# Rotation, local attentions and feed-forward stages of a two-layer block written as one program on each engine

## Chip, cores and metric

One core of a Trainium2 chip runs the whole kernel. The metric is the device time of one execution in microseconds (us), of which the median over several runs is compared. The engines are PE (TensorE, matmuls), DVE (VectorE), ACT (ScalarE), POOL (GpSimd) and SP, which here only issues DMAs. Each has its own queue of instructions that it runs in order, and waits in it on semaphores.

## What is computed

The input x is (2, 1024, 256), so 2 batches of T = 1024 tokens with D = 256 features. A first layer (a 16-head attention and a mixture of 64 experts) makes x1. Then x1 goes through a rotation, which is one 256 x 256 matrix, and through two local transformer layers, and is added again. The change touches only this second half:

```python
for l in range(2):                      # _L1_ffn_ref, q/k scales and norm weights left out
    h = shift_token(x)                  # second half of the features comes from the token before
    q, k, v = split(h @ wqkv[l], 3)     # 8 heads of 64
    q, k = rotary_xpos(l2norm(q), l2norm(k))
    o = local_attention(q, k, v)        # windows of 128: a window sees itself and the one before
    x = x + o @ wo[l]
    h = shift_token(x)
    h = (h - mean(h)) / sqrt(var(h) + 1e-5) * lg + lb
    a, g = split(h @ w1[l] + b1[l], 2)  # 682 value columns, 682 gate columns
    x = x + (a * gelu(g)) @ w2[l] + b2[l]
```

## The kernel before

The second half is five stages, each a block of its own: `stage_rotate` (line 1222), `stage_attention1` for layer 0 (line 1331), `stage_ffn1` for layer 0 (line 1716), and the two again for layer 1. At the end of a block every engine waits for all others, so no instruction of a stage starts before the last of the stage before it. Tokens lie in `xr`, features on the partitions, with one zero column ahead of each batch, so that `shift_token` is only an offset.

**Precision.** Products that need it are split: an operand is a high part (rounded to fp32r) and a low part (what is left), and three matmul products (`PRODUCTS`: high*high, high*low, low*high) make one. So a weight has to be split by copying to the low tile on ACT, subtracting on POOL or DVE, and rounding on ACT (lines 1199 to 1219 for `wqkv`).

**Rotation.** For 16 tiles t of 128 tokens, DVE scales the output of the experts (`r_on`, line 1267), PE transposes it (line 1294), DVE adds it to the input (`r_x1T`, line 1273). After every fourth tile, PE multiplies a block of 512 tokens by the rotation (`rotate`, line 1285), and ACT copies it to `xr` (line 1311). Besides this ACT and POOL split `wqkv` of layer 0 (lines 1203, 1211, 1219), POOL scales the rotary tables (line 1327), and SP writes x1 to HBM in 4 parts (line 1249), which the last stage reads again.

**Attention.** There are 16 windows (NG) of 128 tokens and 20 slots t. Five windows are in work in a slot, in an order written out by hand for each engine. In slot t:
- PE: `rows_of(t-2)` (transposes of q and k, line 1482), `queries_keys(t)` (12 matmuls, line 1460), `scores(t-2, 0)`, `prob_rows(t-3, 0..1)` (line 1506), `mixed(t-4)` (output projection, line 1525), `values(t)` (6 matmuls, line 1460), `prob_rows(t-3, 2..3)`, `scores(t-2, 1)` (line 1497), `weighted(t-3)` (line 1516).
- ACT: q, k and output copies, `w_qkr` (line 1571) and `w_sq` (line 1573) out of the bank of q and k, exponentials (line 1588), a square root of norms in odd slots (line 1597).
- DVE: masked maxima (line 1663), sums of squares (line 1646), `w_sinp` (the sine term, line 1640), copies of transposed probabilities (line 1676), the residual add (line 1681), the split of tokens `w_hst` (lines 1631 and 1633).
- POOL: `w_cosp` (line 1420), `w_turned` (lines 1429 and 1435), the scaling of the probabilities (line 1413).

PE can't start `rows_of(0)` before window 0 has been through the whole chain PE, ACT, DVE and POOL, and POOL normalises windows 0 and 1 together, after both.

**Feed-forward.** Four units (2 batches, 2 halves) of 512 tokens, in a loop over the batches. A unit is 6 hidden tiles f of 128 columns, each with a gate and a value half of 6 matmuls (line 1855), then 36 matmuls of w2 (line 1869). The 682 columns are padded to 768, so there are 12 column tiles. The norm of the unit that follows is made beside it: a matmul for the mean and one for the variance on PE (lines 1833 and 1837), `m_xc` (line 1943), reciprocals `m_rs` (line 1948) and rounding (line 1965) on DVE, squares (line 1886), root `m_sd` (line 1891) and scaling (line 1897) on ACT, and `m_xn` and the low part (lines 1803 and 1806) on POOL. The last unit of a layer makes such a norm too, of a unit that nothing uses. The first unit's norm is made at the start of the stage, with PE waiting. There ACT and DVE split w1 (lines 1901, 1958) and POOL splits w2 (lines 1809, 1811). In layer 0, ACT and POOL then split `wqkv` of layer 1, ahead of the first gelu (line 1921) in ACT's order.

Of the kernel before, what the change touches and what calls it, by code (L numbers as in the profile page):

```python
# [22 lines left out]
F32 = mybir.dt.float32  # L23
# [5 lines left out]
ds = bass.ds  # L29
# [37 lines left out]
HIDP = FT * P  # L67
QK_SCALE = 8.0
# [1120 lines left out]
def load_ffn1(sp, G, A, l):  # L1189
    sp.dma_start(G["w1"][:, :, :], A["w1"][l].rearrange("(k p) n -> p k n", p=P)).then_inc(G["ld_ffn"], 16)  # L1190
    sp.dma_start(G["w2"][:, :, :], A["w2"][l].rearrange("(k p) n -> p k n", p=P)).then_inc(G["ld_ffn"], 16)
    for name in ("lg", "lb", "b1", "b2"):
        sp.dma_start(G[name][:, :], A[name][l]).then_inc(G["ld_ffn"], 16)


LD_ATT, LD_FFN = 32, 96


def copy_wqkv(nc, act, G, l):

    act.wait_ge(G["ld_att"], LD_ATT * (l + 1))
    for k in range(KD):
        nc.scalar.activation(G["wqkv1"][1][:, k, :], G["wqkv1_raw"][:, k, :], ACT.Copy).then_inc(G["wqkv_copy"], 1)


def split_wqkv(nc, pool, G, l):

    low = G["wqkv1"][1]
    for k in range(KD):
        pool.wait_ge(G["wqkv_copy"], KD * l + k + 1)  # L1210
        nc.gpsimd.tensor_tensor(low[:, k, :], G["wqkv1_raw"][:, k, :], low[:, k, :].bitcast(F32),
                                ALU.subtract).then_inc(G["wqkv_low"], 1)


def round_wqkv(nc, act, G, l):

    for k in range(KD):
        act.wait_ge(G["wqkv_low"], KD * l + k + 1)
        nc.scalar.activation(G["wqkv1"][0][:, k, :], G["wqkv1_raw"][:, k, :], ACT.Copy).then_inc(G["wqkv_high"], 1)


def stage_rotate(nc, G, A):


    with ExitStack() as ctx:
        sb = lambda n, s, dt=F32: ctx.enter_context(nc.sbuf_tensor(n, s, dt))
        sem = lambda n: ctx.enter_context(nc.semaphore("r_" + n))
        PB, ident, xr = G["PB"], G["ident"], G["xr"]
        TILES = B * TT
        x1T = sb("r_x1T", [P, KD, N])  # L1230
        rden = sb("r_rden", [P, TILES])
        on = sb("r_on", [P, 2, D])
        step, on_ready, t_ps, x1_done, rot_ps, rot_out, zeroed = (sem(n) for n in (
            "step", "on_ready", "t_ps", "x1_done", "rot_ps", "rot_out", "zeroed"))
        ld_x = [sem(f"ld_x{n}") for n in range(N // HALF)]
        with nc.Block() as block:
            @block.sync
            def _(sp):
                for n in range(N // HALF):
                    ts = slice(n * HALF, (n + 1) * HALF)  # L1240
                    sp.dma_start(x1T[:, :, ts], A["xT"].rearrange("(k p) n -> p k n", p=P)[:, :, ts]).then_inc(ld_x[n], 16)
                load_attention1(sp, G, A, 0)
                sp.dma_start(G["mask"][:, :], A["mask"]).then_inc(G["ld_tab"], 16)
                sp.dma_start(G["qks"][:, :, :, :], A["qks"]).then_inc(G["ld_tab"], 16)
                load_tables(sp, G, A)
                for n in range(N // HALF):
                    ts = slice(n * HALF, (n + 1) * HALF)
                    sp.wait_ge(x1_done, 4 * n + 4)
                    sp.dma_start(G["x1"].rearrange("(k p) n -> p k n", p=P)[:, :, ts], x1T[:, :, ts]).then_inc(G["x1_out"], 16)
                sp.wait_ge(G["x1_out"], 16 * (N // HALF))  # L1250

            @block.gpsimd
            def _(pool):
                nc.gpsimd.memset(xr[:, :, :, 0:1], 0.0).then_inc(zeroed, 1)
                split_wqkv(nc, pool, G, 0)
                scale_tables(nc, pool, G, 0)

            @block.vector
            def _(dve):
                V = nc.vector  # L1260
                link = chain(dve, step)
                link(V.reciprocal(rden[:, :], G["den"][:, :]))
                for t in range(TILES + 1):
                    if t < TILES:
                        if t >= 2:
                            dve.wait_ge(t_ps, t - 1)
                        V.tensor_scalar_mul(on[:, t % 2, :], G["O"][:, t, :], rden[:, t:t + 1]).then_inc(on_ready, 1)
                    if t >= 1:
                        r = t - 1
                        if r * P % HALF == 0:  # L1270
                            dve.wait_ge(ld_x[r * P // HALF], 16)
                        dve.wait_ge(t_ps, r + 1)
                        V.tensor_tensor(x1T[:, :, r * P:(r + 1) * P],
                                        PB[0][:, HALF * (r % 2):HALF * (r % 2) + D].rearrange("p (k t) -> p k t", k=KD),
                                        x1T[:, :, r * P:(r + 1) * P], ALU.add).then_inc(x1_done, 1)

            @block.tensor
            def _(pe):
                def rotate(n):
# [899 lines left out]
```

## Time and profile before

| | us |
|---|---|
| median of 3 runs | 1647.94 |
| lowest and highest | 1646.35, 1648.55 |
| the profiled execution | 1648.95 |
| its span, first to last instruction | 1647.2 |
| mean granted TensorE clock | 0.969 of full speed |

The span is divided by the profile into busy and idle time of each engine. A line of the timeline gives start, duration, engine, line of the kernel, output and inputs, and how many instructions were merged in it. In brackets stands how long the engine was idle before it, and which instruction ended that. The second half of the kernel begins at about 869 us of the span, the attention of layer 0 at 904, its feed-forward at 1141, the attention of layer 1 at 1274, and its feed-forward at 1513.

### The profile page before, as it was taken

To read this page: it belongs to the slowest core of one execution; us is meant where nothing else is said; L and a number is where in the kernel's file an instruction comes from. 1 tells how busy PE (TensorE), PEld (TensorE's weight loads), DVE (VectorE), ACT (ScalarE), POOL (GpSimd) and SP (SyncE) were. 2 spreads that over 40 slices of the span, in tenths; PEclk is the share of its full clock that TensorE was granted. 3 is DMA by queue.
4 is the path that set the end of the run, shared out by engine and by line. 5 is a ranking of instruction groups with operands and counts; after the bars stand their busy time and mean duration, and the time that the engine had idled before them with its cause. 6 is when DMAs were issued, how large, how long until landed. Compare 5 with 4: busy or idle time off the path is not lost. (4 is left out here: it accounts for less than half of the span.)

```text
span 1647.2 us, 24889 instructions
## 1 busy us (share of the span) xinstructions
PE 1498.2 (91%) x9060; PEld 983.4 (60%) x9060; DVE 1050.9 (64%) x1915; ACT 903.6 (55%) x1870; POOL 503.4 (31%) x313
## 2 busy tenths in 40 slices
PE   8889999999986999999996699997799699997898
PEld 3432222222234888888883477775677577775676
DVE  3768888888637656565654456555777455555786
ACT  5147777777751434343432577775443577776342
POOL 7100000000015100000002587774412587774223
PEclk9999999999999999999998899999899799999899
DMA  8831212200000330303006100003000100000010
GB/s 245 141 39 20 34 26 40 40 2 1 11 14 12 120 104 13 103 13 103 0 0 191 55 1 1 1 2 77 1 1 4 54 1 1 2 1 26 4 48 26
DMA packets 59472, 64.98 MB, mean 39 GB/s; under 512 B 15154, under 2 KB 48706, under 8 KB 59380
## 3 DMA queue, kind: packets, MB, share of 16 engines
q1 hardware_dynamic: 58020, 60.37, 14.7%
q10 hardware_dynamic: 1360, 3.41, 0.6%
q8 instruction: 55, 0.90, 0.2%
q14 instruction: 37, 0.30, 0.1%
HBM read 53.08 MB, written 10.49 MB: 39 GB/s over the span
## 5 line engine op out<-in xcount | busy, mean ns | idle before, releaser
L578 DVE TENSOR_REDUCE mcol<-bank 128x1 f32<-128x1024 f32 x256 | 301.8, 1217 | 58.0 <-PE bank L569 58.0
L666 ACT ACTIVATE a_pt<-bank 128x512 f32<-128x512 f32 x512 | 266.1, 603 | 88.2 <-PE bank L698 88.2
L698 PE MATMUL bank<-qa,ka 99*128 99x512 bf16 x512 | 192.9, 384 | 7.6 <-ACT a_pt L666 3.8
L569 PE MATMUL bank<-ka,qa 96*128 96x512 bf16 x512 | 192.4, 383 | 6.4 <-DMA ka<-k_parts 2.9
L1663 DVE CUSTOM_DVE_ANT_0 w_sm<-bank,mask 128x256 f32<-128x256 f32 (+1 forms) x256 | 89.0, 404 | 147.6 <-PE bank L1497 147.6
L1855 PE MATMUL bank<-m_hn,m_w 128*128 128x512 f32 x576 | 150.9, 419 | 19.0 <-DVE m_hn L1986 16.4
L1460 PE MATMUL bank<-wqkv,w_hst 128*128 128x512 f32 x576 | 156.6, 420 | 12.5 <-DVE w_sinp L1640 7.6
L698 PEld LDWEIGHTS bank<-qa,ka 99*128 99x128 bf16 x512 | 49.1, 98 | 165.1 <-ACT a_pt L666 120.7
L1855 PEld LDWEIGHTS bank<-m_hn,m_w 128*128 128x128 f32 x576 | 112.3, 195 | 56.1 <-issue 27.2
L709 PE MATMUL bank<-a_pt,vst 128*32 128x512 f32 x1024 | 136.4, 605 | 0.1
L1588 ACT ACTIVATE w_sm<-w_sm,w_st 128x256 f32<-128x256 f32 (+1 forms) x256 | 124.0, 489 | 19.2 <-DVE w_st L1663 19.0
L1460 PEld LDWEIGHTS bank<-wqkv,w_hst 128*128 128x128 f32 x576 | 109.6, 199 | 37.6 <-issue 14.9
L1413 POOL TENSOR_TENSOR w_sm<-w_sm,w_st 128x1024 f32<-128x1024 f32 (+1 forms) x64 | 114.8, 1794 | 37.3 <-DVE w_st L1670 37.3
L1064 PE MATMUL bank<-f_y,f_ET 128*128 128x256 f32 x768 | 108.6, 290 | 0.7 <-DVE f_y L1163 0.7
L615 POOL COPY vst<-v 128x512 f32<-128x512 f32 x8 | 4.9, 612 | 334.8 <-PE bank L709 278.2
L1064 PEld LDWEIGHTS bank<-f_y,f_ET 128*128 128x128 f32 x768 | 96.1, 191 | 3.9 <-issue 1.6
L1420 POOL TENSOR_TENSOR w_cosp<-w_qkr,cosT 128x1024 f32<-128x1024 f32 x32 | 75.9, 2373 | 67.0 <-ACT w_qkr L1571 67.0
L1021 PE MATMUL bank<-phi,X0T 128*128 128x512 f32 x384 | 92.1, 394 | 3.9 <-PEq L765 3.9
L995 PE MATMUL bank<-f_th,X 128*128 128x512 f32 x384 | 90.3, 389 | 0.0
L1429 POOL TENSOR_TENSOR w_turned<-w_cosp,w_sinp 128x1024 f32<-128x1024 f32 x32 | 75.7, 2366 | 43.5 <-issue 34.0
L569 PEld LDWEIGHTS bank<-ka,qa 96*128 96x128 bf16 x512 | 49.6, 98 | 62.6 <-DVE mcol L578 11.5
L1021 PEld LDWEIGHTS bank<-phi,X0T 128*128 128x128 f32 x384 | 73.0, 191 | 19.8 <-issue 4.7
(236 smaller groups left out, 2688.8 us busy)
## 6 DMA issues: line engine op xcount, KB each, us to landing
f_wex<-in_W SPq DMA_DIRECT2D x8, 2048.0 KB, 12.0
qa<-q_parts SPq DMA_DIRECT2D x48, 128.0 KB, 4.8
ka<-k_parts SPq DMA_DIRECT2D x48, 128.0 KB, 5.1
q_parts<-p_parts SPq DMA_DIRECT2D x16, 192.0 KB, 3.2
k_parts<-p_parts SPq DMA_DIRECT2D x8, 384.0 KB, 3.5
wqkv_raw<-in_wqkv SPq DMA_DIRECT2D x2, 1536.0 KB, 8.7
w<-in_w SPq DMA_DIRECT2D x2, 1536.0 KB, 6.5
phi<-in_phi SPq DMA_DIRECT2D x5, 512.0 KB, 3.7
```

Of the source, the lines that this page charges most:

```text
L569: last = nc.tensor.matmul(max_bank(G, r)[:, jh * HALF:(jh + 1) * HALF], G["qa"][k][0:KS, hg % 2, h, it * P:(it + 1) * P], G["ka"][k][0:KS, ...
L578: nc.vector.reduce_max(G["mcol"][hg % 2][:, p:p + 1], max_bank(G, r)[:, :], X).then_inc(G["max_free"], 1)
L666: nc.scalar.activation(pt[n % 2][:, q, :], sbank(HG * step + q), ACT.Exp, scale=HD0 ** -0.5).then_inc(p_ready, 1)
L698: mm(sbank(i), ka[k][:, q, n * P:(n + 1) * P], qa[k][:, ih, q, :], start=True, stop=True).then_inc(st_ps, 1)
L709: last = mm(obank[32 * q:32 * q + 32, :], vst[hg // 2 % 2][:, jt, q, :], pt[jt % 2][:, q, :], start=(jt == 0), stop=(jt == TT - 1))
L995: last = mm(PB[2 + b][:, k * HALF:(k + 1) * HALF], X0[cx][:, b * TT + mt, k * P:(k + 1) * P], ths[ct][:, mt % 2, :], start=(mt == n == 0), ...
L1021: last = mm(logit_bank(mt)[:, b * HALF:(b + 1) * HALF], X0T[cx][:, k, b * T + mt * P:b * T + (mt + 1) * P], phis[cp][:, k, :], start=(n == ...
L1064: last = mm(PB[1][:, HALF * (t % 2):HALF * (t % 2) + D], ETs[ce][:, t % 2, n, :], ys[cy][:, n, t // TT, :], start=(n == i == 0), stop=(n = ...
L1413: V.tensor_tensor(sm[:, i % 2, hs, keys(i)], sm[:, i % 2, hs, keys(i)], st[:, i % 2, 3, hs].unsqueeze(2).to_broadcast([P, 4, 2 * WIN if i ...
L1460: last = mm(out, hst[:, i // 2 % 2, ch, k, (i % 2) * P:(i % 2 + 1) * P], wqkv[cw][:, k, j * INNER:(j + 1) * INNER], start=(n == k == 0), s ...
L1588: last = S(sm[:, i % 2, h, keys(i)], sm[:, i % 2, h, keys(i)], ACT.Exp, bias=st[:, i % 2, 1, h:h + 1], scale=-1.0, accum_out=st[:, i % 2, ...
L1855: last = mm(PB[2 + f % 2][:, part * HALF:(part + 1) * HALF], w1s[cw][:, k, col + f * P:col + (f + 1) * P], hns[ch][:, hf, k, :], start=(n ...
```

## The change

The five stages become one block, `stage_layers`, with one written-out program on each engine and no loop instructions. The parts:
- Windows 0 and 1 of layer 0 (`EARLY_SLOTS` = 2) are projected among the rotation's tiles, after tiles 9 and 13. Those of layer 1 are projected inside the last unit of the feed-forward of layer 0. The attention program then begins at slot 2.
- The norm of a layer's first unit is made in slots 15 to 19 of its attention. No norm is made beside the last unit.
- w1 and w2 are split in 3 pieces within the attention's slots 5 to 11 (ACT copies in slots 5 to 7, POOL subtracts in 7 to 9, ACT rounds in 9 to 11). DVE no longer takes part in it. `wqkv` of layer 1 is split after units 0 and 1.
- The last 42 value and 42 gate columns of w1 share one tile of 128 columns, so a unit has 11 column tiles instead of 12.
- Values are kept for 5 windows and keys for 2, in rings. The mask has three parts, so that an odd and an even window find their keys in the ring's order.
- Loads of the following layer's weights and tables are issued by SP after waits on what read the ones before. x1 is read again, and the output stored, a half at a time.

```diff
+VRING = 5
+EARLY_SLOTS = 2
...
+        def w1_cols(f):
+            return (WHOLE * P + f * P, f * P) if f < WHOLE else (2 * WHOLE * P,)
...
             @block.gpsimd
...
                     for t in SLOTS1:
...
+                        if 7 <= t < 7 + NPIECES:
+                            low_piece(l, t - 7)
...
+                attention(0)
+                normalise(0)
+                normalise(1)
+                for k in range(KD):
+                    low_qkv(1, k)
+                normalise(2)
+                for i in range(4):
+                    scale_table(1, i)
+                normalise(3)
+                attention(1)
...
             @block.tensor
...
+                    for t in SLOTS1[first:]:
+                        if there(t - 2):
+                            rows_of(t - 2)
+                        if there(t):
+                            queries_keys(l, t)
+                        if t == NG:
+                            pe.wait_ge(qk_sb, before(NG))
+                            pe.wait_ge(sin_done, before(NG))
+                            means(UNITS * l)
...
+                        if there(t - 3):
+                            prob_rows(t - 3, 2)
+                            prob_rows(t - 3, 3)
+                        if t == NG:
+                            variances(UNITS * l)
+                        if there(t - 2):
+                            scores(t - 2, 1)
...
+                def feed_forward(l):
+                    for n in range(UNITS):
...
+                        for f in range(FT):
...
+                            if ahead and f in (1, 3):
+                                queries_keys(l + 1, f // 2)
+                            if ahead and f in (2, 4):
+                                values(l + 1, f // 2 - 1)
+                        pe.wait_ge(y_done, KD * u)
+                        if ahead:
+                            pe.wait_ge(qk_sb, NG * (l + 1) + EARLY_SLOTS)
+                            pe.wait_ge(sin_done, NG * (l + 1) + EARLY_SLOTS)
...
+                for t in range(TILES):
+                    turn_rows(t)
+                    if t % 4 == 1 and t >= 4:
+                        rotate(t // 4 - 1)
+                    if t in (9, 13):
+                        queries_keys(0, t // 4 - 2)
+                        values(0, t // 4 - 2)
+                rotate(TILES // 4 - 1)
+                pe.wait_ge(x1_done, TILES)
+                pe.wait_ge(rot_out, KD * (N // HALF))
+                pe.wait_ge(G["x1_out"], 16 * (N // HALF))
+                attention(0, EARLY_SLOTS)
...
             @block.scalar
...
+                        if t == NG:
+                            squares(UNITS * l)
...
+                        if 5 <= t < 5 + NPIECES:
+                            copy_piece(l, t - 5)
+                        if 9 <= t < 9 + NPIECES:
+                            round_piece(l, t - 9)
+                        if t == NG + 1:
+                            deviation(UNITS * l)
+                        if t == NG + 2:
+                            scaled(UNITS * l)
...
+                for n in range(N // HALF):
+                    if n == 1:
+                        copy_qkv(0)
+                    rotated(n)
+                    if n == 1:
+                        round_qkv(0)
+                    if n >= 2:
+                        queries_keys(0, n - 2)
+                        values(0, n - 2)
+                norms(0, 0)
...
             @block.vector
...
+                        if t == NG:
+                            centred(UNITS * l)
...
+                        if t == NG - 1:
+                            tile_sums(UNITS * l)
...
+                        if t == NG:
+                            square_sums(UNITS * l)
+                        if there(t - 3):
+                            prob_rows(t - 3, 2)
...
+                        if t == NG + 2:
+                            for q in range(2):
+                                inverse(UNITS * l, q)
+                    high(UNITS * l)
...
+                    if t == 9:
+                        dve.wait_ge(zeroed, 1)
+                        split_tokens(0, 0)
+                    if t == 13:
...
+                        squared_norms(0, 0)
+                        sines(0, 0)
+                split_tokens(0, 1)
+                squared_norms(0, 1)
+                sines(0, 1)
+                inverse_norms(0, 0)
```

Names of the new program that the diff shows: `rotated(n)` is ACT's copy of a rotated block, `queries_keys` on ACT makes `w_qkr` and `w_sq`, `deviation` is the root `m_sd`, `inverse` the reciprocals `m_rs`, `scaled` makes `m_hn`, and `high` and `normalise` make its two parts.

## Rows read from the trace of the kernel before

**Rows 1.** Page, part 1: busy time of PE, share, instructions.

```profile
PE 1498.2 (91%) x9060; PEld 983.4 (60%) x9060; DVE 1050.9 (64%) x1915; ACT 903.6 (55%) x1870; POOL 503.4 (31%) x313
```

**Rows 2.** Windows of 25 us: length; busy us of PE, PEld, DVE, ACT, POOL; clock; DMA.

```profile
975.00:1000.00 25.00, 24.70 (x204) 20.23 (x204) 13.76 (x47) 19.31 (x49) 18.82 (x10) 1.00 0.01 2
...
1225.00:1250.00 25.00, 25.00 (x105) 19.51 (x104) 18.82 (x25) 9.57 (x13) 5.47 (x4) 1.00 0.00 0
```

**Rows 3.** The chain that ended last, feed-forward of layer 1: start, us, what.

```profile
1530.84 5.24 PE bank L1855 x12
...
1560.18 2.80 PE bank L1855 x12
...
1563.84 8.39 PE bank L1855 x36
...
1589.87 0.86 PE bank L1833 x2
```

**Rows 4.** Timeline of PE, feed-forward of layer 0 and start of layer 1.

```profile
1158.84 5.22 PE L1855 MATMUL bank<-m_hn,m_w 128*128 128x512 f32 x12 [8.20 <-DVE m_hn L1986]
...
1170.28 7.41 PE L1855 MATMUL bank<-m_hn,m_w 128*128 128x512 f32 x24 [2.56 <-DVE m_hid L1997]
...
1192.38 2.96 PE L1855 MATMUL bank<-m_hn,m_w 128*128 128x512 f32 x12
...
1246.16 2.96 PE L1855 MATMUL bank<-m_hn,m_w 128*128 128x512 f32 x12
...
1275.80 5.99 PE L1460 MATMUL bank<-wqkv,w_hst 128*128 128x512 f32 x18 [2.59 <-DVE w_hst L1633]
...
1298.27 1.97 PE L1482 MATMUL bank<-ident,w_turned 128*128 128x128 f32 x8 [7.29 <-POOL w_turned L1435]
```

**Rows 5.** Timelines of DVE, ACT and POOL, end of layer 1's attention and the norms after.

```profile
1507.29 0.69 DVE L1676 COPY w_PT<-bank 128x512 f32<-128x512 f32 x1
...
1515.30 1.28 DVE L1943 TENSOR_TENSOR m_xc<-xr,bank 128x512 f32<-128x512 f32 x2 [1.38 <-PE bank L1833]
...
1523.40 3.37 DVE L1948 RECIPROCAL m_rs<-m_sd 128x256 f32<-128x256 f32 x2 [1.08 <-ACT m_sd L1891]
...
1516.02 1.23 ACT L1886 ACTIVATE m_sq<-m_xc 128x512 f32<-128x512 f32 x2 [1.52 <-DVE m_xc L1943]
...
1552.76 2.73 POOL L1803 TENSOR_TENSOR m_xn<-m_xc,m_rs 128x512 f32<-128x512 f32 x2 [34.00 <-DVE m_rs L1948]
```

**Rows 6.** Timeline of ACT in a unit of layer 0: a table load and what follows.

```profile
1179.29 1.28 ACT L1921 ACT_TABLE_LOAD   x1
1180.59 0.69 ACT L1921 ACTIVATE m_gl<-bank,b 128x512 f32<-128x512 f32 x1
```

**Rows 7.** Timeline of PE, rotation and first slots of layer 0.

```profile
884.07 3.60 PE L1285 MATMUL bank<-r_x1T,rot 128*128 128x512 f32 x8
...
905.74 4.43 PE L1460 MATMUL bank<-wqkv,w_hst 128*128 128x512 f32 x18 [2.30 <-DVE w_hst L1633]
...
926.98 1.97 PE L1482 MATMUL bank<-ident,w_turned 128*128 128x128 f32 x8 [7.62 <-POOL w_turned L1435]
```

**Rows 8.** Timelines of POOL, DVE and ACT in the same stretch.

```profile
885.24 6.87 POOL L1211 TENSOR_TENSOR wqkv<-wqkv_raw,wqkv 128x1536 fp32r<-128x1536 f32 x2 [15.94 <-ACT wqkv L1203]
...
922.73 2.34 POOL L1429 TENSOR_TENSOR w_turned<-w_cosp,w_sinp 128x1024 f32<-128x1024 f32 x1 [1.31 <-DVE w_sinp L1640]
925.02 3.76 POOL L1435 TENSOR_TENSOR w_turned<-w_turned,w_rn 128x1024 f32<-128x1024 f32 x2
...
889.09 3.17 DVE L1267 TENSOR_SCALAR r_on<-O,r_rden 128x256 f32<-128x256 f32 x1
...
912.01 1.22 DVE L1640 TENSOR_TENSOR w_sinp<-bank,sinT 128x1024 f32<-128x1024 f32 x1
...
899.21 2.85 ACT L1219 ACTIVATE wqkv<-wqkv_raw 128x1536 fp32r<-128x1536 f32 x2
...
908.80 1.02 ACT L1571 ACTIVATE w_qkr<-bank 128x1024 f32<-128x1024 f32 x1 [4.73 <-PE bank L1460]
```

More of the change, by code:

```diff
@@ L1193, in load_ffn1, with load_tables @@
         sp.dma_start(G[name][:, :], A[name][l]).then_inc(G["ld_ffn"], 16)
+def load_tables(sp, G, A):
+    for i in range(4):
+        sp.dma_start(G["tab"][i % 2][:, :, i // 2, :], A["tables"][i].rearrange("(w p) d -> p w d", p=P)).then_inc(G["ld_tables"], 16)
 LD_ATT, LD_FFN = 32, 96
[L1199 to L1203, printed above, removed]
@@ L1206, in split_wqkv @@
[L1206 to L1219, printed above, removed]
@@ new lines, in _ @@
+                V.memset(xr[:, :, :, 0:1], 0.0).then_inc(zeroed, 1)
+                V.memset(mean[:, :], 1.0 / D).then_inc(consts, 1)
+                V.memset(eps[:, :], LN_EPS).then_inc(consts, 1)
+                pool.wait_ge(consts, 2)
+                for k in range(KD):
+                    low_qkv(0, k)
+                for i in range(4):
+                    scale_table(0, i)
+                attention(0)
+                normalise(0)
+                normalise(1)
+                for k in range(KD):
+                    low_qkv(1, k)
@@ L1301, in _ @@
-            @block.scalar
-            def _(act):
-                for n in range(N // HALF):
-                    if n == 1:
-                        copy_wqkv(nc, act, G, 0)
-                    if n == 3:
-                        round_wqkv(nc, act, G, 0)
-                    for m in range(KD):
-                        act.wait_ge(rot_ps, KD * n + m + 1)
-                        c0 = 1 + (n % 2) * HALF
-                        nc.scalar.activation(xr[:, m, n // 2, c0:c0 + HALF], PB[1 + m][:, 0:HALF],
-                                             ACT.Copy).then_inc(rot_out, 1)
-                act.wait_ge(zeroed, 1)
@@ L2018, in program @@
+                feed_forward(0)
+                attention(1, EARLY_SLOTS)
+                feed_forward(1)
 def program(nc, A, out):
@@ L2038, in program @@
         G["early_sem"] = early_sem
-        layer_sems = {}
-        def layer_sem(n):
-            if n not in layer_sems:
-                layer_sems[n] = top.enter_context(nc.semaphore(n))
-            return layer_sems[n]
-        G["layer_sem"] = layer_sem
         G["ident"] = sb("ident", [P, P])
@@ L2122, in constants @@
     i, j = np.arange(WIN)[:, None], np.arange(WIN)[None, :]
-    c["mask"] = np.concatenate([np.where(j >= i, 0.0, MASKED), np.where(j <= i, 0.0, MASKED)], 1).astype(f)
+    last, own = np.where(j >= i, 0.0, MASKED), np.where(j <= i, 0.0, MASKED)
+    c["mask"] = np.concatenate([last, own, last], 1).astype(f)
     c["ident"] = np.eye(P, dtype=f)
```

1311 lines of the change are left out of this document (661 added, 650 removed).

## Prediction

> **What bounds the kernel now.** I read the page first: PE is busy 1498.2 of 1647.2 us, the next engine 1050.9 [rows 1]. So time is gained by fewer matmuls or by less idling of PE, and I looked for both in the second half, which the change alone touches. The windows show two kinds of steady work. In a slot of the attention PE has 24.70 of 25 us, while ACT has 19.31 and POOL 18.82 and so some 6 us each to spare. In a unit of the feed-forward PE has all of 25.00 and DVE 18.82 [rows 2]. The chain of waits confirms it for the last stage: PE and nothing else from 1530.84 on, one unit after another [rows 3]. PE idles where the stages meet. That is read from PE's timeline, from landmark to landmark: from the transposes of window 0 back to the block before. These landmarks, not busy shares, carry the sum.
>
> **Fewer matmuls.** 36 matmuls of one kind take 8.39 us, or 0.233 each [rows 3]. A unit loses 6 of them, 1.40 us. The last unit of each layer loses the matmuls for a mean and a variance too, 2 x 0.86 = 1.72 [rows 3]. Seven units here (the eighth is in the next part) give 7 x 1.40 + 1.72 = 11.5 gained. PE is the bound in them, so it counts in full.
>
> **From feed-forward 0 to attention 1.** Before, unit 3 starts at 1246.16 and the first transposes of window 0 at 1298.27 [rows 4]: 52.1 us, in which the two early slots take 36 matmuls (8.4 us if PE is never throttled) and the rest is the round through ACT, DVE and POOL. After, the unit holds 66 + 36 + 36 matmuls of 0.233 = 32.2. I follow its queues. The two projections come after tiles 1 and 3. ACT takes `w_qkr` and `w_sq` between gelus (1.02 each), DVE the sums of squares and the sine term (1.22 each) behind the hidden parts of tiles 2 and 4 [rows 8]. The second projection waits for the first sine term, which comes in time. The w2 matmuls use its bank, and wait for the second: projection ends, ACT 2.0, DVE's tile 4 and 2.4 more. I get 1.5 us of stall. Behind the last w2 matmul stay one residual add and a reciprocal on DVE (1.1) and one POOL multiplication, half of 3.76 [rows 8]: 3.1. Sum 36.8, so 15.3 gained.
>
> **Unit 0 of layer 0.** It takes 33.54 us before (1158.84 to 1192.38), with PE idle 2.56 us at 1170.28 [rows 4], because the gelu stands behind the split of `wqkv` in ACT's queue. The same unit of layer 1 takes 1560.18 - 1530.84 = 29.34 [rows 3]. The split moves behind the unit, so 4.2 are gained. What is late next is the split itself: POOL's two subtractions (6.87 together [rows 8]) now run in the first tiles of unit 1, beside DVE.
>
> **The norm in the last slots.** Before, unit 0's norm stands in the open, begun only when the attention is over, and the unit of layer 1 starts at 1530.84 [rows 3]. After, four things are queued behind new work.
> 1. Slot 16: the variance matmuls wait for centring 1.28, squares 1.23 and their sum, and the second half of the scores is behind them. Between 0.9 (the matmuls alone) and 3.2 (all in the open) I take 2.4, since maxima and exponentials share those queues.
> 2. Slot 17: a table load and the root, 1.28 + 0.69 [rows 6], ahead of the output copy of window 14, on which PE's projection waits: 2.0.
> 3. Slot 18: so the probability copy that ends at 1507.98 [rows 5] ends at 1512.4. Then come the reciprocals, 3.37, and POOL's two products, 2.73: 1518.5.
> 4. ACT's scaling stands ahead of the output copy of window 15. Scaling 0.8, copy 0.6, projection 2.05 and residual add 0.4 give 1522.4. Only then come DVE's rounding and POOL's low parts: 3.1, so the unit starts at 1525.7.
>
> That is 5.1 earlier than 1530.84. Layer 0 ends in the same orders, so 10.2 for both. The bounds for each are 0 (the norm costs the slots what it saves) and 12 (steps 1 and 2 hidden, 4.4, and copy, projection and add, 3.0, not behind the scaling).
>
> The table load is where a page speaks against this. The trace shows 1.28 us and the next activation 0.02 us behind it, though the load starts at once after work [rows 6]. The Trainium skill, ScalarE: Activation LUTs, section "What ACT_TABLE_LOAD costs", adds a drain of about 1.38 us to every switch; by it step 2 would be 3.4 us instead of 2.0, and the sum 2.8 smaller over two layers. I go by the row.
>
> **Early slots among the rotation.** This looks like a gain and is, by the queues, a loss. Before, PE is through with block 1 of the rotation at 887.7, and the first transposes of window 0 run at 926.98 [rows 7]. After:
> - The first projection stands behind tile 9, but needs `wqkv` split: POOL is done at 892.1 and ACT's rounding 1.4 later [rows 8], so 893.5. PE has idled 6 us. In the trace 18 matmuls take 4.43 us after a short idle time, 5.99 after others, and 12 take 5.22 after 8.20 idle [rows 4, 7]. I take 6.6, to 900.1.
> - Tiles 10 to 13 and block 2: 6, to 906.2. ACT copies block 2 before q and k, 0.7, then 2.0. DVE's squares and sine term 2.4: 911.4. The second projection waits for that.
> - Projection 6, tiles 14 and 15 with DVE's adds 1.8, block 3 3.6 [rows 7]: 922.9.
> - ACT block 3 0.7, q and k 2.0, DVE 2.6; POOL's sum 2.34 and product 1.9 [rows 8]: 932.4.
>
> So 5.5 us lost. The bounds are 2 (PE keeps its clock) and 8. The write of x1 isn't the last wait: its last DMA starts when tile 15 is added, about 919, so it has 13 us. Before, the same DMA, tiles 10 to 15 and two blocks all fitted between 887.7 and 905.74 [rows 7].
>
> **Splitting the weights inside the slots.** Per layer POOL gets 3 subtractions of up to 3.4 us and ACT 6 copies of up to 1.45, for which I use the `wqkv` rows of 1536 columns [rows 8]. Each slot gets one of a kind. Their cover is the idle quarter of both engines [rows 2], and what they delay (probabilities, q and k copies) is used half a slot later. At nothing they would cost 0; with no cover, 2 x (3 x 3.3 + 6 x 1.4) = 37. I take 1 us a layer: 2 lost.
>
> **The port.** DVE's scaling `r_on` took 3.17 us instead of 0.34 because POOL's subtraction ran [rows 8]. In unit 1, DVE's casts meet POOL's two. PE waits only for the first of DVE's three steps of a tile, from PSUM, so 1 us is lost. The Trainium skill, GPSIMD Engine Reference, section "Specifications", says that POOL shares its SBUF interface with DVE; the row agrees.
>
> **Sum.** 11.5 + 15.3 + 4.2 + 10.2 - 5.5 - 2 - 1 = 32.7 us gained. The profiled execution took 1648.95, so 1616.3; it is 1.0 above the median of 1647.94, which gives 1615.3.
>
> **Rivals.**
> - *Norm and early slots hide fully.* If ACT's scaling doesn't hold up window 15 and steps 1 and 2 are hidden, each norm gives 7.4 more, and if the early slots fit in PE's waits the 5.5 are not lost: 20.3 more, 1595. For it speaks that waits that I add one behind another may overlap. Against it, the orders on ACT. Chance 0.15.
> - *The ends are given back.* The norm's steps lengthen the last slots by all they save (10.2 less), and the rotation costs 8 (2.5 more): 1628. Chance 0.18.
> - *The splits are on the path (the slower side).* POOL and ACT close a ring with PE in each slot. The place is slots 5 to 11, and the port makes DVE late too. With no cover the cost is 37 instead of 2: 1650. It decides slower above 2.1 us per piece, for 18 pieces. The spare 6 of 25 us [rows 2] speak against it. Chance 0.04.
> - *The early slots do not do what they say.* If the bank that q, k and w2 share makes PE wait in unit 3 for both rounds through ACT and DVE, 2 x (2.0 + 2.4) come on top, 8.8: 1624. Chance 0.08.
>
> My forecast has 0.55. The range, 1602 to 1630, holds the forecast, its own bounds, the second and fourth rival, and leaves out the first and third. A measurement of this kernel tells 0.2% (3.3 us) from no change. Below 1644.6 lie all cases but the third and something unseen: faster 0.94, same 0.02, slower 0.04.
>
> **What would show it.** In the profile after: w1 matmuls 528 instead of 576; units of about 25.5 us; window 0's transposes of layer 1 about 37 us after the start of unit 3; those of layer 0 later than 927, with PE idle before the first projection for `wqkv`; feed-forward starts 5 us earlier after the last slot, with PE waiting for ACT's output copy in front of the last projection. The prediction is wrong if slots 5 to 11 are longer than the others, if w2 waits long for a sine term, or if PE's clock falls inside a unit.

## Result and the profile after

The changed kernel takes 1633.86 us (median of 4 runs, 1631.24 to 1635.53). The kernel before takes 1647.24 beside it (4 runs, 1646.35 to 1648.55). The ratio is 0.9914, with an interval of 0.9901 to 0.9926. So it is faster, as forecast, but by 13.4 us instead of 32.7, and 1633.86 lies above the forecast range of 1602 to 1630.

First the page of the changed kernel, part 1, which answers to [rows 1], and its windows, which answer to [rows 2]. The first window is one slot of layer 0 that stands out.

```profile
PE 1493.2 (92%) x9004; PEld 975.4 (60%) x9004; DVE 1028.7 (63%) x1879; ACT 897.9 (55%) x1854; POOL 514.6 (32%) x313
```

```profile
1020.00:1037.00 17.00, 14.66 (x109) 11.84 (x106) 11.57 (x27) 11.81 (x28) 15.70 (x8) 0.90 0.01 1
975.00:1000.00 25.00, 24.15 (x202) 19.73 (x202) 13.69 (x48) 21.37 (x48) 20.24 (x10) 1.00 0.01 2
1225.00:1250.00 25.00, 24.85 (x103) 18.53 (x102) 20.21 (x29) 9.62 (x13) 5.47 (x4) 1.00 0.00 1
```

PE's busy time fell by 5.0 us only, and it is still the bound nearly everywhere. In the slot that stands out, slot 9, PE is idle for 2.3 of 17 us, its mean clock is 0.90 and POOL is busy for 15.70. The experiments e4 and e5 look for the reason.

The profiled execution took 1631.24 (span 1629.5), 17.7 less than the 1648.95 before. It is the fastest of its four runs. I divided the 17.7 by landmarks of PE's timeline, those of the prediction:

| stretch | before | after | gained | forecast |
|---|---|---|---|---|
| start to the rotation's first transposes | 869.93 | 867.79 | 2.1 | 0 |
| from there to window 0's transposes | 57.05 | 60.95 | -3.9 | -5.5 |
| to window 14's, both layers | 370.7 | 377.4 | -6.7 | -2 |
| window 14's to unit 0, both layers | 93.7 | 88.7 | 5.1 | 10.2 |
| layer 0, unit 0 to unit 3 | 87.32 | 83.45 | 3.9 | 7.4 |
| unit 3 to window 0's transposes | 52.11 | 38.79 | 13.3 | 15.3 |
| layer 1, unit 0 to the last w2 matmuls | 101.46 | 97.93 | 3.5 | 7.3 |
| from there to the end | 14.9 | 14.5 | 0.4 | 0 |

The first 2.1 us lie ahead of anything that changed. They are no effect of it: another execution of the changed kernel reached the same point at 869.69. Without them the trace shows 15.6, and five of the seven forecasts are too high. One profiled execution gives such a stretch to about 1 us: the norm's stretch, for one, takes from 43.4 to 45.0 us a layer in the eight profiled executions whose program is the same there. Here is PE's timeline of the changed kernel. These lines answer to [rows 7]:

```profile
881.65 3.60 PE L1524 MATMUL bank<-r_x1T,rot 128*128 128x512 f32 x8
891.42 6.04 PE L1539 MATMUL bank<-wqkv,w_hst 128*128 128x512 f32 x18 [6.18 <-ACT wqkv L1716]
...
908.02 6.22 PE L1539 MATMUL bank<-wqkv,w_hst 128*128 128x512 f32 x18 [5.09 <-DVE w_sinp L1910]
...
928.74 1.94 PE L1567 MATMUL bank<-ident,w_turned 128*128 128x128 f32 x8 [9.73 <-POOL w_turned L1463]
...
1031.54 1.94 PE L1590 MATMUL bank<-ident,w_sm 128*128 128x128 f32 x8 [2.34 <-DVE w_PT L1983]
1033.41 1.83 PE L1581 MATMUL bank<-w_kT,w_qT 64*128 64x256 f32 x8
...
1271.93 9.18 PE L1681 MATMUL bank<-m_hid,w 128*128 128x512 f32 x36 [2.00 <-DVE w_sinp L1910]
1284.26 1.97 PE L1567 MATMUL bank<-ident,w_turned 128*128 128x128 f32 x8 [3.15 <-POOL w_turned L1463]
...
1497.95 2.79 PE L1609 MATMUL bank<-w_oT,wo 128*128 128x128 f32 x16 [2.21 <-ACT w_oT L1792]
1500.54 1.91 PE L1590 MATMUL bank<-ident,w_sm 128*128 128x128 f32 x8
...
1509.54 3.56 PE L1609 MATMUL bank<-w_oT,wo 128*128 128x128 f32 x16 [5.16 <-ACT w_oT L1792]
1517.07 5.49 PE L1659 MATMUL bank<-m_hn,w 128*128 128x512 f32 x12 [3.97 <-POOL m_hn L1425]
...
1563.51 9.53 PE L1681 MATMUL bank<-m_hid,w 128*128 128x512 f32 x36
```

The reader is to see six things. The projections among the rotation wait for `wqkv` and for the first sine term (891.42, 908.02). Slot 9 has an idle time that the kernel before did not have, and its next two groups run slowly (1031.54, 1033.41; the same groups take 1.06 and 1.13 in other slots). In unit 3, w2 waits 2.00 us for a sine term. Both late output projections wait for ACT's `w_oT` and are slow (2.79, 3.56). w2's 36 matmuls, which I had at 8.4, take 9.53. And the feed-forward of layer 1 starts at 1517.07.

ACT's timeline at the end of layer 1's attention shows what the last two projections wait for:

```profile
1495.43 1.28 ACT L1768 ACT_TABLE_LOAD   x1
1496.73 0.69 ACT L1768 ACTIVATE m_sd<-bank,m_eps 128x512 f32<-128x512 f32 x1
1497.31 0.59 ACT L1792 ACTIVATE w_oT<-bank 128x512 f32<-128x512 f32 x1
...
1508.20 0.82 ACT L1776 ACTIVATE m_hn<-m_xn,lb,lg 128x512 f32<-128x512 f32 x1 [0.36 <-POOL m_xn L1422]
1508.92 0.58 ACT L1792 ACTIVATE w_oT<-bank 128x512 f32<-128x512 f32 x1
```

Window 14's copy stands behind the table load and the root, window 15's behind the second scaling, though its data were ready at 1504.4.

### The profile page after: what moved, and what is told of

It is laid out like the page before. It is cut to its first block and busy times, and to the rows that moved or that the text cites. A ratio compares the mean times of both kernels' runs of the same rounds, so it can differ in the third digit from the quotient of the medians.

```text
span 1629.5 us, 24376 instructions
## 1 busy us (share of the span) xinstructions
PE 1493.2 (92%) x9004; PEld 975.4 (60%) x9004; DVE 1028.7 (63%) x1879; ACT 897.9 (55%) x1854; POOL 514.6 (32%) x313
## 5 line engine op out<-in xcount | busy, mean ns | idle before, releaser
L1659 PE MATMUL bank<-m_hn,w 128*128 128x512 f32 x528 | 137.1, 416 | 8.0 <-issue 4.0
L1659 PEld LDWEIGHTS bank<-m_hn,w 128*128 128x128 f32 x528 | 102.0, 195 | 39.2 <-issue 12.2
L1848 ACT ACTIVATE m_gl<-bank,b 128x512 f32<-128x512 f32 (+1 forms) x48 | 33.1, 689 | 104.3 <-PE bank L1659 104.3
L1590 PE MATMUL bank<-ident,w_sm 128*128 128x128 f32 x480 | 68.9, 288 | 20.5 <-DVE w_PT L1983 20.5
```

Of the source, the lines that this page charges most:

```text
L1590: last = tr(T_PS[p % 2][:, c0:c0 + P], sm[:, i % 2, 2 * p + e, j * P:(j + 1) * P], ident[:, :])
L1659: last = mm(PB[2 + f % 2][:, part * HALF:(part + 1) * HALF], w1s[cw][:, k, col:col + P], hns(u)[:, ch, k, :], start=(i == k == 0), stop=(i ...
```

## Experiments

Unless it is said otherwise, each is one edit of the changed kernel. The gain is given against the first run here, and every median can be off by about 1 us. All kernels before measured beside them had medians of 1647.1 to 1648.1.

| run | median us | ratio to before | gain |
|---|---|---|---|
| changed kernel again | 1631.55 | 0.9901 [0.9886, 0.9916] | |
| e1 full rows | 1629.06 | 0.9886 [0.9869, 0.9902] | 2.5 |
| e2 half tiles grouped | 1629.94 | 0.9894 [0.9877, 0.991] | 1.6 |
| e3 copy before scaling | 1621.33 | 0.9843 [0.9827, 0.986] | 10.2 |
| e4 subtract in odd slots | 1625.38 | 0.9864 [0.9848, 0.9881] | 6.2 |
| e5 subtract in even slots | 1628.28 | 0.9881 [0.9866, 0.9896] | 3.3 |
| e6 no early slots in layer 0 | 1626.43 | 0.9876 [0.9861, 0.9891] | 5.1 |
| e7 = e1 + e3 + e4 + e6 | 1605.93 | 0.9742 [0.9729, 0.9755] | 25.6 |
| e8 full rows and grouped | 1628.74 | 0.989 [0.9875, 0.9905] | 2.8 |
| e9 = e3 + earlier reciprocals | 1620.45 | 0.9837 [0.9821, 0.9852] | 11.1 |
| e10 = e7 + e8 + earlier reciprocals | 1604.4 | 0.9733 [0.972, 0.9747] | 27.2 |
| e11 = e10 + earlier variance | 1601.07 | 0.9719 [0.9706, 0.9732] | 30.5 |

**The changed kernel again**, without an edit, as the level for the others.

> The changed kernel itself, with nothing altered, beside the runs that follow. It shows how far its time moves between sessions: 1633.9 us was measured first, and sums over its landmarks in one profiled execution say some 1631. A time of 1630 to 1634 is expected; the gains of the other kernels are read against both.

It took 1631.55 (1630.79 to 1633.37). Slot 9 takes 17.02 and 16.94 us in it (17.02 and 16.92 in the first profile), and the middle units 26.6. The pattern is the program's, not one execution's.

**e1: w2's last hidden tile in 128 rows.** The tile of the last 42 columns has 64 rows in the changed kernel. Here PE and DVE take 128. The rows of w2 that the other 64 meet are zero, so they add nothing to the sum.

```diff
-mm(..., w2s[cw][value_rows(f), f, m * P:(m + 1) * P], hids[ch][value_rows(f), f, :], ...)
+mm(..., w2s[cw][:, f, m * P:(m + 1) * P], hids[ch][:, f, :], ...)
...
-v, s, r = FT * u + f, f % 2, value_rows(f)
+v, s, r = FT * u + f, f % 2, slice(0, P)
```

> The last hidden tile goes through w2 with all 128 rows (the upper 64 meet zero weights) instead of 64. Theory, switch: a matmul of 64 rows next to one of 128 keeps the weight load from running beside the matmuls, and this makes 36 w2 matmuls take 9.5 us instead of 8.4. Then each unit of the feed-forward is 1.05 us shorter (unit 1 of layer 1: 26.6 to 25.5) and the kernel 8.4 us faster. Rival, late tile: w2 waits for DVE's last hidden tile. Then it stays at 9.5 and the time doesn't move.

It gave 2.5 us, not 8.4. Middle units went from 26.60 to 26.20. The weight loads of the changed kernel show why anything was gained:

```profile
1569.40 0.54 PEld L1681 LDWEIGHTS bank<-m_hid,w 128*128 128x128 f32 x3 [0.58 <-DVE m_hid L2040]
1570.30 0.52 PEld L1681 LDWEIGHTS bank<-m_hid,w 64*128 64x128 f32 x3 [0.37 <-issue]
1571.18 0.53 PEld L1681 LDWEIGHTS bank<-m_hid,w 128*128 128x128 f32 x3 [0.36 <-issue]
1572.07 0.53 PEld L1681 LDWEIGHTS bank<-m_hid,w 64*128 64x128 f32 x3 [0.37 <-issue]
1572.96 0.19 PEld L1659 LDWEIGHTS bank<-m_hn,w 128*128 128x128 f32 x1 [0.36 <-issue]
```

Three loads of 64 rows take as long as three of 128 (0.52, 0.53). But at each change of the row count the next load starts 0.37 us late, behind no wait. So the smaller tile saves no load time here and costs at its borders. The Trainium skill, TensorE: Matmul & The Clock Gate, section "LDWEIGHTS (loading the stationary operand)", says that the time of a load depends on its columns, not its rows; the rows agree. The first line shows a second loss, a wait for DVE. In e1 it is still there (PEld's timeline of e1):

```profile
1570.17 2.62 PEld L1681 LDWEIGHTS bank<-m_hid,w 128*128 128x128 f32 x12 [0.60 <-DVE m_hid L2040]
```

**e2: w2 in three groups**, so that the 64-row matmuls stand together and the last wait comes later.

```diff
-for tiles in (range(FT - 2), range(FT - 2, FT)):
+for tiles in (range(FT - 2), range(FT - 2, FT - 1), range(FT - 1, FT)):
```

> Still 64 rows, but the six matmuls of 64 rows stand together at the end of a unit, so there are 2 changes of row count per unit instead of 4. If the price is per change, w2 falls from 9.5 to 9.0 us and the kernel is 4 us faster. If it is per matmul of 64 rows (0.18 us on each of 6), nothing moves. If the last tile was late, nothing moves either.

It gave 1.6. w2 takes 8.74 instead of 9.53 and its wait is gone, yet the unit takes 26.18: PE now waits at the next unit's start, for POOL's low part of the norm (0.29 at 1571.85). Middle units can't separate the two losses, since e1 and e2 both end at 26.2. Unit 3 of layer 0 can: there w2 starts 2.00 us after the matmuls before it, behind a sine term, and never waits for the last hidden tile. In the changed kernel w2, with three changes of the row count inside it, takes 9.18. PE's timelines of e1 (no change) and e2 (one change):

```profile
1273.26 8.61 PE L1681 MATMUL bank<-m_hid,w 128*128 128x512 f32 x36 [2.00 <-DVE w_sinp L1910]
```

```profile
1273.59 8.81 PE L1681 MATMUL bank<-m_hid,w 128*128 128x512 f32 x36 [2.01 <-DVE w_sinp L1910]
```

That is 0.2 us for each change. So of the 9.53 in a middle unit some 0.6 are the three changes, and by difference to 8.5 some 0.4 the wait for DVE (an estimate).

**e3: window 15's output copy ahead of the norm's scaling on ACT.**

```diff
-                        if t == NG + 2:
+                        if t == NG + 3:
                             scaled(UNITS * l)
```

> ACT's scaling of the first norm moves behind the output copy of window 15 (slot 19 instead of 18). Theory, ACT's queue: PE idles 5.1 us before the last output projection because the copy stands behind the scaling. Then the projection starts some 7 us earlier, and the unit starts when the low parts are ready, 5 us earlier in each layer: 10 us faster in all. Rival, the norm's own chain (reciprocals, products, scaling, rounding, low parts) ends no earlier: the projection moves, the unit starts at most 1 us earlier, and the time gains 2 us or less.

It gave 10.2, as much as expected. PE's timeline of e3 at the end of layer 1's attention:

```profile
1494.46 2.05 PE L1609 MATMUL bank<-w_oT,wo 128*128 128x128 f32 x16 [2.21 <-ACT w_oT L1792]
1496.35 1.04 PE L1590 MATMUL bank<-ident,w_sm 128*128 128x128 f32 x8
1497.32 1.97 PE L1600 MATMUL bank<-w_PT,w_vsb 128*64 128x128 f32 x32
1499.98 2.05 PE L1609 MATMUL bank<-w_oT,wo 128*128 128x128 f32 x16 [0.70 <-ACT w_oT L1792]
1507.20 4.52 PE L1659 MATMUL bank<-m_hn,w 128*128 128x512 f32 x12 [5.17 <-POOL m_hn L1425]
```

From window 14's transposes to unit 0 it takes 39.00 and 37.91 instead of 44.36 and 44.30. The wait of 5.16 before the last projection is 0.70, and the projection takes 2.05 instead of 3.56. Copy, projection and residual add no longer stand between the scaling and the rounding.

Not all of this is the order. PE's granted clock also fell in the changed kernel and not in e3. These are windows of the changed kernel and then of e3; the clock is the third value from the end:

```profile
1492.75:1497.95 5.20, 2.99 (x42) 2.58 (x40) 2.24 (x10) 4.59 (x12) 3.25 (x2) 1.00 0.00 0
1497.95:1502.40 4.45, 4.45 (x26) 4.12 (x26) 1.19 (x3) 0.44 (x1) 0.00 (x0) 0.63 0.02 4
```

```profile
1489.26:1494.46 5.20, 2.99 (x42) 2.58 (x40) 2.24 (x10) 4.58 (x12) 3.25 (x2) 1.00 0.00 0
1494.46:1497.30 2.84, 2.84 (x24) 2.69 (x24) 0.74 (x2) 0.44 (x1) 0.00 (x0) 1.00 0.03 6
```

The work ahead is the same in both, to the hundredth on PE. Then the changed kernel runs at a mean of 0.63 and e3 at 1.00. This first fall is no effect of the order: e7, which has e3's order, has it too (2.73 and 1.91 us for the same two groups), and its stretch to unit 0 is 39.02 in layer 1, 1.1 more than e3's. The last projection is another matter. In the changed kernel it follows 5.16 us of idle time and its clock is 0.54 (1509.50 to 1513.00); in e3 and e7 it follows 0.70 us and takes 2.05. So the order gives 5.3 of the 6.4 us in layer 1.

In unit 3 of layer 0, which e3's edit does not touch, e3 loses 1.6: the clock falls inside w2, which takes 10.76 us at 1266.97. In e4, e5, e6 and e9 this stretch is as long as in e3 (40.4 from unit 3's start to window 0's transposes, changed kernel 38.8). So up to some 2 us of any single gain can be where the clock falls.

**e4 and e5: POOL's subtractions of w1 and w2 in every second slot** instead of the neighbouring slots 7, 8 and 9; ACT's roundings move with them. In e4 they are in odd slots, behind the scaling of two windows of q and k on POOL, in e5 in even ones.

```diff
-                        if 7 <= t < 7 + NPIECES:
-                            low_piece(l, t - 7)
+                        if t in (7, 9, 11):
+                            low_piece(l, (7, 9, 11).index(t))
...
-                        if 9 <= t < 9 + NPIECES:
-                            round_piece(l, t - 9)
+                        if t in (9, 11, 13):
+                            round_piece(l, (9, 11, 13).index(t))
```

(e5 has 8, 10, 12 and 10, 12, 14.)

> POOL's three subtractions per layer stand after slots 7, 9 and 11 instead of 7, 8 and 9 (ACT's roundings after 9, 11 and 13). Slot 9 took 17.0 us instead of 13.6 in each layer. Theory, pile-up or collision behind the subtraction of slot 8: with none there slot 9 falls back to 13.6 and the kernel is 6.8 us faster. Rival, each subtraction has a price wherever it is: the 3.4 us are only spread over more slots and the time stays within 2 us.

> POOL's three subtractions stand after slots 8, 10 and 12, one slot apart from each other, each after an even slot. Theory, phase: after an even slot a single subtraction moves POOL's cosine product of the odd slot onto the small DVE operation w_nsq, which needs the shared port (it took 1.99 us instead of 0.18), and the probability copies behind it make PE wait. Then slots 9, 11 and 13 each take up to 3.4 us more, and the kernel is 10 to 14 us slower than with subtractions after odd slots. Rival, pile-up: only two subtractions in neighbouring slots are too much for POOL; then the time is that of the odd placement.

e4 gave 6.2: slot 9 takes 13.64 again, and no slot from 5 to 13 shows a cost of the splits. e5 gave 3.3, between the theories: slot 9 takes 14.10 and slot 13 takes 14.39, instead of one slot of 17.02. DVE's and POOL's timelines of the changed kernel, slots 8 and 9:

```profile
1026.43 1.22 DVE L1916 TENSOR_REDUCE w_ss<-w_sq 128x16 f32<-128x1024 f32 x1
1027.67 1.99 DVE L1919 TENSOR_SCALAR w_nsq<-w_ss 128x32 f32<-128x32 f32 x1
1029.58 1.21 DVE L1910 TENSOR_TENSOR w_sinp<-bank,sinT 128x1024 f32<-128x1024 f32 x1
1030.72 0.68 DVE L1983 COPY w_PT<-bank 128x512 f32<-128x512 f32 x1
```

```profile
1021.79 3.65 POOL L1416 TENSOR_TENSOR w<-w_raw,w 128x1408 fp32r<-128x1408 f32 x1
1025.39 1.90 POOL L1440 TENSOR_TENSOR w_sm<-w_sm,w_st 128x1024 f32<-128x1024 f32 x1
1027.24 2.39 POOL L1449 TENSOR_TENSOR w_cosp<-w_qkr,cosT 128x1024 f32<-128x1024 f32 x1
```

After PE's wait of 2.34 in slot 9 the clock falls too (window of the changed kernel, clock 0.55):

```profile
1031.50:1035.20 3.70, 3.66 (x18) 2.79 (x18) 1.26 (x4) 1.67 (x2) 3.70 (x3) 0.55 0.00 0
```

And the same DVE and PE groups in e4:

```profile
1030.74 0.18 DVE L1919 TENSOR_SCALAR w_nsq<-w_ss 128x32 f32<-128x32 f32 x1
```

```profile
1032.79 1.06 PE L1590 MATMUL bank<-ident,w_sm 128*128 128x128 f32 x8 [0.53 <-DVE w_PT L1983]
1033.79 1.13 PE L1581 MATMUL bank<-w_kT,w_qT 64*128 64x256 f32 x8
```

With two subtractions in neighbouring slots POOL doesn't catch up, and its `w_cosp` (1027.24) falls on DVE's `w_nsq`, an instruction of 32 elements on each partition. That takes 1.99 instead of 0.18 and ends when POOL's instruction ends (1029.6). Everything behind it on DVE is 1.8 late, the copy `w_PT` too. PE waits 2.34 instead of 0.53, and its next two groups, at the lower clock, lose another 0.88 and 0.70. The sum is 1.81 + 1.58 = 3.4, the whole excess of slot 9. In e5 `w_nsq` takes 0.64 and PE's wait is 0.99, with no slow matmuls behind. So most of the loss is the pile-up (2.2 of the 3.4 us in a layer, by the slots), and the rest is in which slots they stand.

**e6: layer 0's first two windows after the rotation, as before.**

```diff
-                    if t in (9, 13):
-                        queries_keys(0, t // 4 - 2)
-                        values(0, t // 4 - 2)
...
-                attention(0, EARLY_SLOTS)
+                attention(0, 0)
```

> The projections of windows 0 and 1 of layer 0 no longer stand among the rotation's tiles; the attention starts at slot 0 after the rotation, as before the change. Theory, ordering on PE and ACT: the early slots cost 3.9 us against the kernel before, so the first transposes of window 0 come 4 us earlier and the kernel is 4 us faster. Rival: in one program they do save something (no stage end in between), then undoing them costs up to 5 us.

It gave 5.1. From the rotation's first transposes to window 0's it takes 56.58, where the changed kernel takes 61.22 in its second profile. The early slots of layer 0 are a loss. The stretch that holds those of layer 1 gains 13.3, but no run takes them out alone.

**e7: e1, e3, e4 and e6 together.**

> All rows for the last w2 tile, the copy before the scaling, subtractions after odd slots and no early slots in layer 0, together. If the four causes are separate, the gains add up: 8.4 + 10 + 6.8 + 4 = 29 us below the changed kernel, 1604 us, near the 1615 that was forecast or below it. If some of them hide each other, it is above 1610.

It took 1605.93. The single gains sum to 24.0, and 25.6 were measured. Within the error of the four medians the gains add up, so no loss hides another.

**e8: e1's and e2's edits together.**

> All 128 rows for the last hidden tile, and the last two tiles of w2 one after the other (24, 6, 6, matmuls of one tile for both output halves) instead of 24 and 12. With all rows alone a middle unit fell from 26.6 to 26.2 us, grouped alone also to 26.2, where 102 matmuls of 0.233 and two pairs of 0.86 make 25.5. Theory, late tile: the rest is PE waiting for DVE's last hidden tile, which comes one half tile (1.4 us) sooner in PE's program than before the change. The six matmuls put in between cover 1.4 us, so units take 25.5 to 25.7 us, and the six middle units give 3 us against all rows alone. Rival: 102 matmuls simply take 0.240 each; then units stay at 26.2.

It gave 2.8, hardly more than e1. PE's timeline of e8:

```profile
1560.62 8.52 PE L1681 MATMUL bank<-m_hid,w 128*128 128x512 f32 x36
1569.66 3.06 PE L1659 MATMUL bank<-m_hn,w 128*128 128x512 f32 x12 [0.53 <-POOL m_hn L1425]
```

w2 is back near its old 8.39, and the unit still takes 26.20. What ends PE's wait points at another chain of this length: the following norm's, from the variance matmuls through root, reciprocals, POOL's products, scaling, rounding and low part. The unit of the kernel before took 26.89, so this chain had some 0.7 us to spare, less than the 1.40 that the unit was to lose. e11 tests this.

**e9: e3, and DVE's reciprocals of the norm half a slot earlier.**

```diff
+                        if t == NG + 2:
+                            for q in range(2):
+                                inverse(UNITS * l, q)
                         if there(t - 4):
                             added(t - 4)
```

> On top of the copy before the scaling, DVE's two reciprocals of the first norm move ahead of the residual add in slot 18, into a stretch in which DVE was idle 3.8 us. Theory, the norm's own chain now sets the start of the unit: it starts 3.65 us earlier minus 0.8 (the add and probability copy are late), about 3 us in each layer, 6 us in all against the copy before the scaling (1621.3 to 1615). Rival, PE's slots: the copy that is delayed holds up PE by as much, and nothing is gained.

It gave 0.9 more than e3, not 6. The reciprocals and POOL's products came earlier, but the rounding hardly did. The stretches to unit 0 are 1.9 and 0.9 us shorter in the profiled execution. DVE's timeline of e9:

```profile
1495.89 0.36 DVE L1988 TENSOR_TENSOR xr<-bank,xr 128x256 f32<-128x256 f32 x1
...
1501.06 0.42 DVE L1988 TENSOR_TENSOR xr<-bank,xr 128x256 f32<-128x256 f32 x1 [4.21 <-PE bank L1609]
1501.39 0.75 DVE L1960 CAST m_hn<-m_hn 128x512 fp32r<-128x512 f32 x2
```

The rounding (1501.39) stands behind window 15's residual add, which waits for PE's last projection. I had left out that queue order.

**e10: e7, e2's grouping and e9's reciprocals.**

> The four edits together (1605.9 us), plus the grouped w2 tiles and the earlier reciprocals. If these two causes are separate from the four, 3 and 6 us come off: 1597 us. If the norm's chain already ran beside something else, only the 3 us: 1603.

It took 1604.4, 1.5 under e7. Middle units stay at 26.2, with PE waiting 0.53 for `m_hn` as in e8.

**e11: e10, with the following norm's variance one hidden tile earlier** (PE's matmuls, ACT's root, DVE's reciprocals).

```diff
-                            if f == 3 and n + 1 < UNITS:
+                            if f == 2 and n + 1 < UNITS:
...
-                                if f in (3, 4):
-                                    inverse(u + 1, f - 3)
+                                if f in (2, 3):
+                                    inverse(u + 1, f - 2)
```

> On top of the kernel with all edits (1604.4 us), the variance matmuls, the root and the reciprocals of the following unit's norm move one hidden tile ahead (after tile 2 instead of 3). There PE's w2 matmuls take 8.4 us again, but each middle unit still takes 26.2 us, and PE waits 0.5 us for POOL's low part of the following norm. Theory, norm chain: the shorter unit leaves the chain from variance to low parts too little time, and this chain now sets the unit's length. With 2.8 us more for it, units take 25.5 to 25.9 us, and six of them give 2 to 4 us: 1601 to 1602. Rival: the wait is only the last step of what PE would lose anyway (weight loads, issue); then units stay at 26.2. A price that may show: the variance now waits up to 0.3 us for the sum of squares.

It took 1601.07 (5 runs, 1598.69 to 1602.75), 3.3 under e10. PE's timeline of e11:

```profile
1515.97 2.96 PE L1659 MATMUL bank<-m_hn,w 128*128 128x512 f32 x12
...
1533.27 8.52 PE L1681 MATMUL bank<-m_hid,w 128*128 128x512 f32 x36
1541.63 2.96 PE L1659 MATMUL bank<-m_hn,w 128*128 128x512 f32 x12
```

A middle unit of layer 1 takes 1541.63 - 1515.97 = 25.66 and waits for nothing. That is the unit I had forecast (25.5). The price shows in unit 1 of layer 0, where POOL splits `wqkv` beside it: PE waits 0.82 for `m_xsum` and 1.32 for `m_sqsum`, and the unit takes 28.09 instead of e10's 27.47. This is the best version, 47 us under the kernel before and 32.8 under the changed one as first measured.

## Why the prediction was right and wrong

The sum was 32.7 and the trace shows 15.6. Of the 17.1 missing, 7.3 are in the units (3.5 and 3.8 in the two layers), 5.1 in the norm, 4.7 in the splits and 2.0 in the way from unit 3 to window 0. The early slots and the end give 2.0 back.

**Fewer matmuls: 1.40 a unit was the wrong size.** The step that failed is "PE is the bound in them, so it counts in full". In layer 1's middle units 26.89 became 26.60, so 0.3 gained. What stood in its place are three things: the changes of the row count (0.2 us each, four in a unit), and two waits that the shorter unit uncovered, for DVE's last hidden tile and for the following norm. Taking away the changes gives 0.4 (e1), taking away DVE's wait and half of the changes gives 0.4 (e2), taking away all of both gives no more (e8), since the unit is then as long as the norm's chain, 26.2. Only with that chain started earlier does it fall by 0.5 more (e11, 25.66). A busy share of PE of 25.00 in 25 [rows 2] says that nothing is late now; it says nothing on how far another chain is from being late. In units without a following norm the step was right: in layer 1's last unit w2 starts 15.44 us after w1 (1615.00 - 1599.56), before 18.50, so 3.06 gained where I had 1.40 + 1.72 = 3.12.

**Splitting the weights: 1 a layer was 3.3.** I weighed each piece against the spare share of a slot [rows 2], one by one. The third rival named the ring and the port but wanted them in all of slots 5 to 11; it happened in slot 9 alone, behind two subtractions in a row. It was this rival's mechanism at a fifth of its price: slot 9 costs 3.4 and 3.3 in the two layers, 6.7 of the rival's 37. e4 shows that my reason (cover enough) holds if the pieces are spaced after odd slots. Slot 15 is 0.6 longer in each layer and stays so in all versions. It now holds the norm's tile sums on DVE, for which I had no term, but no run takes them out. In layer 1 the slot of window 0's transposes is 1.0 shorter, so the stretch comes to 6.7 all the same.

**The norm in the last slots: 2.5 a layer instead of 5.1.** The order of the steps was right. Step 1 was 2.4, as forecast (slot 16 takes 12.29, before 9.90). In step 2 the load and the root took 1.28 and 0.69, and in step 4 ACT's scaling did hold up window 15's copy; e3 gives that back. What failed is PE's time in steps 3 and 4, which I took at full clock. The first late projection and the transposes behind it take 2.79 and 1.91 instead of e3's 2.05 and 1.04, so DVE's probability copy starts 3.68 us after the projection (1501.63 - 1497.95), in e3 2.53. The last projection takes 3.56 instead of 2.05. That is 1.15 + 1.51 = 2.7 in layer 1, about the 2.6 a layer that are missing. The 1.51 go with the idle time of 5.16 that the order makes, and e3 and e7 have them back. The 1.15 do not: e7 pays them too. (The sum itself had a slip: 1522.4 and 3.1 make 1525.5, not 1525.7, 0.2 a layer.) On the page that spoke against the change (the Trainium skill, ScalarE: Activation LUTs, "What ACT_TABLE_LOAD costs", with its drain of 1.38): the root starts 1.30 us after the load's start (1495.43 to 1496.73), so there is no such drain here.

**Early slots among the rotation: a loss, as forecast,** -3.9 against -5.5. The first projection waits for `wqkv` 6.18 where I had 6. It and the second take 6.04 and 6.22, where I had 6.6 and 6. The rest of the chain was 1.6 shorter than worked out. e6 confirms sign and size: taking them out shortens this stretch by 4.6.

**Unit 0 of layer 0 and unit 1.** Unit 0 takes 29.34 against 33.54: the 4.2 for the queue order are right, the 1.4 for its matmuls did not come. Unit 0 of layer 1 takes 29.29, no less than before, with 9.4 from w2 to the next unit and the first 12 matmuls at 5.49 (a clock of 0.50, before 5.24). In e11 both take 27.3, so the 1.4 can come. Unit 1 takes 27.49, 0.9 above unit 2: forecast 1. Beside POOL's subtractions of `wqkv` DVE's `m_xsum` takes 2.80 (at its shortest 0.68) and PE waits 0.67 for it, which speaks for the port; no run moves them.

**Feed-forward 0 to attention 1: 13.3 of 15.3.** The waits were right: 2.00 before w2 where I had 1.5, and 3.15 before the transposes where I had 3.1. Of the 1.5 left most are w2's row counts again (9.18 instead of 8.4) and 0.28 for the first sine term, the rest is in small pieces.

**The rivals.** "The ends are given back" gave 1628 and is the nearest, but half right: of the 5.1 a layer 2.6 were given back, to PE's clock and not to the norm's steps, and the rotation cost less than I had, not more. Four terms failed in the same direction, and the range, 1602 to 1630, had no case in which several do. Of the signs that I had named for a wrong prediction two came: slot 9 is longer than the others, and PE's clock is 0.50 at the start of unit 0. The latter was so before as well (1530.84 to 1534).

## What to carry to other kernels

When a loop body gets shorter, list every chain that ran beside it with its length: the gain ends at the longest of them. Where engines wait for each other in a ring, as in a slot here, work put into the spare time of one is to be spaced, since one piece may fit and two in a row not. Where an engine has something that PE waits for in its queue, put it ahead of anything that is only needed later; here one such order was worth 10.2 us in two layers. Judge a gain of 1 or 2 us by the slots or units that the edit touches, not by the whole time.

## What the runs showed of the hardware

- A small DVE instruction can take as long as what POOL is doing. `w_nsq` took 1.99 instead of 0.18 and ended with POOL's `w_cosp`. In e5 a cast of 128 x 512 took 3.51 us (0.43 elsewhere in the kernel) beside a subtraction of 3.23 that began with it, and ended 0.3 us behind it. These are DVE's and POOL's timelines of e5:

```profile
1022.33 3.51 DVE L1898 CAST w_hst<-xr 128x512 fp32r<-128x512 f32 x1
```

```profile
1022.32 3.23 POOL L1416 TENSOR_TENSOR w<-w_raw,w 128x1408 fp32r<-128x1408 f32 x1
```

- PE's granted clock was 0.50 (1.2 of 2.4 GHz) from 1500.50 to 1502.40 and 0.55 on average from 1031.50 to 1035.20, behind idle times of 2.21 and 2.34 us; before these it was 1.00. Idle time alone does not tell it: after the same 2.21 us e3 kept 1.00, with the same work ahead of it, and its projection took 2.05 instead of 2.79. What makes the difference stays open.
- Matmuls of 64 rows between such of 128 start their weight load 0.37 us late at each change, in both directions, and cost PE 0.2 us at each (w2 in 9.18, 8.81 and 8.61 us with three, one and no change inside). Nothing in the trace names the cause.
